# A mixture of experts with its matmuls turned, and gathers that leave out empty places

## The chip, the core and the metric

The kernel runs on one core of a Trainium2 chip. The metric is the device time of one execution in microseconds (us). TensorE (PE) multiplies and transposes, VectorE (DVE) and ScalarE (ACT) work on tiles element by element, GpSimd (POOL) here mostly issues indirect transfers, and SyncE (SP) issues the other transfers. SBUF is the on-chip memory of 128 partitions; PSUM is the memory that TensorE writes, in eight banks of 128 x 512 f32. A matmul has a stationary operand, which is loaded first, and a moving operand, whose columns stream past it.

## The reference, cut to what matters

The whole is a decoder of two layers on 4 x 256 tokens of width 256. The change lies in the feed-forward part of the first layer, a mixture of 64 experts: each token goes to the 6 experts with the largest scores, and every token also goes through one shared expert.

```python
E, K, H, F_EXP = (64, 6, 256, 176)
def _swiglu(x, g, v, o):
    return jax.nn.silu(x @ g) * (x @ v) @ o
scores = jax.nn.softmax(x @ w_router.T, axis=-1)
topw, topi = jax.lax.top_k(scores, K)
combine = jnp.zeros((T, E), x.dtype).at[jnp.arange(T)[:, None], topi].add(topw)
# over all experts: acc + cw[:, None] * _swiglu(x, g, v, o)
shared = _swiglu(x, swg, swv, swo)
return (routed + shared).reshape(b, s, h)
```

So 1024 x 6 = 6144 pairs of token and expert are worked. All of it is f32.

## The kernel before

The program is one block with a stream of instructions written out for each engine; counting semaphores hold the streams together. Up to the mixture the kernel does the first attention and a state-space scan; behind it come the rest of the first layer and the second layer.

The pairs are sorted into blocks of 128 places. Each expert owns at least one block, an expert with more than 128 tokens gets further ones behind. Four blocks make a group (`NJ = 4`). The first 16 groups (`FIXED`) hold block e of expert e; a loop behind them works the groups of overflow, of which this input has one. So 17 groups, or 68 blocks, are worked.

For a block, POOL gathers 128 rows of 1 KB from the normalized tokens in DRAM (`gather`, one row for each place, by the table `tok_of`; a place that no token fills reads row 0). TensorE turns the tile (`turn_g`, two transposes), ACT copies it to `xgT`. `gate_up` has the activations stationary and the weights moving: two matmuls of 352 columns give gate and value of 128 tokens, tokens on partitions. ACT takes a tanh of the gate, DVE's `hidden` makes silu(gate) x value out of it in two instructions. The result has tokens on partitions, and the down projection needs the hidden units there, so `turn_hid` transposes it (two transposes of 88 units), ACT copies it back, and `down` runs two matmuls of 256 columns. DVE copies the product to `y_out`, and SP stores it block by block to `y_dram`. The 68 blocks' rows are gathered from there, weighted and added later.

The weights stream in. SP has a ring of two groups: `load_block` for block j of group i + 2 is issued when block j of group i has been copied out, right behind the store of that block:

```python
for j in range(NJ):
    store_y(d * RING + r, j)
    sp.wait_ge(w_loaded[j], at(d, 32 * RING, 32 * (r + RING)))
    sp.sem_inc(load_due, 1)
    load_block(d * (RING * NJ) + ((r + RING) * NJ + j), j, w_gv[:, r * NJ + j], w_dn[:, r * NJ + j])
```

A block's weights are one transfer of 352 KB (`w_gv`) and one of 192 KB (`w_dn`, 96 partitions with 2 KB each, of which 88 carry data). The gather of group i + 2 is issued behind the turn of group i + 1, which TensorE does within group i. The engines also carry work of a later part within the groups (`side`, `rotate_key`).

Of the kernel before, what the change touches and what calls it, by code (L numbers as in the profile page):

```python
# [12 lines left out]
ALU = mybir.AluOpType  # L13
# [20 lines left out]
FH = F // 2  # L34
FP = 96
# [99 lines left out]
ACT_STEPS = 1 + PAIRS + 1  # L135

# [18 lines left out]
def build(nc, a, out):  # L155

    with ExitStack() as ctx:
# [124 lines left out]
        tok_id = sb("tok_id", [P, TILES])  # L282
        tri_bf = sb("tri_bf", [P, P], BF16)
# [51 lines left out]
        w_gv = sb("w_gv", [P, RING * NJ, KD, 2 * F])  # L335
        w_dn = sb("w_dn", [FP, RING * NJ, 2, D])
        y_out = sb("y_out", [P, NJ, D])
        g_th = sb("g_th", [P, NJ, F])
        hid = sb("hid", [P, NJ, F])
        hidT = sb("hidT", [FH, NJ, 2 * P])  # L340
        xg = sb("xg", [P, NJ, D])
        xgT = sb("xgT", [P, NJ, KD * P])
        sh_gv = sb("sh_gv", [P, KD, 2 * F])
        sh_dn = sb("sh_dn", [FH, 2, D])
# [130 lines left out]
        x_stored = sem("x_stored")  # L475
        gathered = [sem(f"gathered{j}") for j in range(NJ)]
        w_loaded = [sem(f"w_loaded{j}") for j in range(NJ)]
        y_stored = [sem(f"y_stored{j}") for j in range(NJ)]
# [3 lines left out]
        gv_ready = sem("gv_ready")  # L482
        g_tanh = sem("g_tanh")
        g_silu = sem("g_silu")
        hid_ready = sem("hid_ready")
        hid_turned = sem("hid_turned")
        hidT_copied = sem("hidT_copied")
# [57 lines left out]
        def pair(n):  # L545
            return ps[:, n:n + 2, :].rearrange("p a b -> p (a b)")

# [6 lines left out]
        def _(sp):  # L554
# [67 lines left out]
            for dst, src in ((w_router, "w_router"), (iota, "iota"), (tok_id, "tok_id"), (tri_bf, "tri_bf")):  # L622
                sp.dma_start(dst[:], a[src]).then_inc(moe_consts, 16)
            for dst, src in ((sh_gv, "sh_gv"), (sh_dn, "sh_dn"), (pos, "pos"), (ident_bf, "ident_bf"),
                             (x_wq, "x_wq"), (x_wo, "x_wo"), (head_sel, "head_sel")):
# [3 lines left out]
            def load_block(e, j, gv, dn):  # L629
                sp.dma_start(gv, a["w_gv"][bass.ds(e, 1)].rearrange("a p k n -> (a p) k n")).then_inc(w_loaded[j], 16)  # L630
                sp.dma_start(dn, a["w_dn"][bass.ds(e, 1)].rearrange("a p k n -> (a p) k n")).then_inc(w_loaded[j], 16)

            for r in range(RING):
                for j in range(NJ):
                    if r:
                        sp.wait_ge(w_loaded[j], 32 * r)
                    load_block(r * NJ + j, j, w_gv[:, r * NJ + j], w_dn[:, r * NJ + j])
# [25 lines left out]
            used = used_groups(sp)  # L663
            with sp.Fori(FIXED, used) as i:
                for j in range(NJ):
                    e = sp.value_load(expert_row[0:1, bass.ds(i * NJ + (j - E), 1)], min_val=0, max_val=E - 1)
                    buf = bass.ds((i & 1) * NJ + j, 1)
                    store_y(i - RING, j)
                    sp.wait_ge(w_loaded[j], at(i, 32, 0))
                    sp.sem_inc(load_due, 1)  # L670
                    load_block(e, j, w_gv[:, buf].rearrange("p a k n -> p (a k) n"),
                               w_dn[:, buf].rearrange("p a k n -> p (a k) n"))
            for r in range(RING):
                for j in range(NJ):
                    store_y(used - RING + r, j)
# [23 lines left out]
        def _(pe):  # L699
# [236 lines left out]
            pe.wait_ge(moe_consts, 64)  # L936
# [8 lines left out]
            def gate_up(j, x_of, w):  # L945

                for k in range(KD):
                    last = mm(ps[:, j, 0:2 * F], x_of(k), w(k), start=(k == 0), stop=(k == KD - 1))  # L948
                last.then_inc(gv_ready, 1)

            def turn_hid(n, j, bk):
                pe.wait_ge(hid_ready, n + 1)
                for f in range(2):
                    last = nc.tensor.transpose(ps[0:FH, bk, f * P:(f + 1) * P], hid[:, j, f * FH:(f + 1) * FH], ident[:])
                last.then_inc(hid_turned, 1)

            def down(n, j, bk, w):
                pe.wait_ge(hidT_copied, n + 1)
                for f in range(2):
                    last = mm(ps[:, bk, 256:512], hidT[:, j, f * P:(f + 1) * P], w(f), start=(f == 0), stop=(f == 1))  # L960
                last.then_inc(down_ready, 1)

            def shared_up(tiles):

                for t in tiles:
                    if t >= NJ:
                        pe.wait_ge(down_copied, t - NJ + 1)
# [1902 lines left out]
```

## Time and profile before

| | |
|---|---|
| three runs | 991.32, 992.77, 993.33 us; median 992.77 us |
| the profiled execution | span 985.7 us from the first to the last instruction; what lies around the span is not in the profile |
| TensorE | busy 870.2 us (88%) |
| VectorE, ScalarE, GpSimd | busy 720.6, 510.4, 407.1 us |
| the loop over the groups | 521.3 us to 698.7 us of the span |
| HBM | read 88.45 MB, written 17.14 MB |

The shares are means over parts with different limits, so the loop is read by itself. There the profile's row of DMA shows 9 tenths or more, and TensorE's row does too.

### The profile page before, as it was taken

Reading aid. Unit: us, or ns where it says so; the run is one execution under the profiler, and the core shown is the slowest. Engines: PE = TensorE matmul, PEld = TensorE weight load, DVE = VectorE, ACT = ScalarE, POOL = GpSimd, SP = SyncE. Lnnn points to the kernel's source line nnn. Section 1 sums busy time; section 2 is a strip of 40 time slices with the busy share of each in tenths; the row PEclk is TensorE's granted clock in tenths of the full one; section 3 lists DMA queues with packets and bytes.
Section 4 is the critical chain, followed back from the end, with each engine's and each line's share of the span. In section 5 each row is a group of like instructions: output and inputs, shape, how many; then the busy total and the mean of one; then the engine's idle time right before and its main releaser. Section 6 shows DMA issues by size and latency. Waiting matters only on the chain.

```text
span 985.7 us, 15418 instructions
## 1 busy us (share of the span) xinstructions
PE 870.2 (88%) x5267; PEld 568.3 (58%) x5271; DVE 720.6 (73%) x1377; ACT 510.4 (52%) x1022; POOL 407.1 (41%) x338
## 2 busy tenths in 40 slices
PE   7999999999999999988889999999546867899886
PEld 3466666666565666656666777677423654343443
DVE  5667786959696867768774556665467798998797
ACT  3563554545544444445444334455522457898485
POOL 0203448494848577534214333333377312221013
PEclk9999999999999999989999999999866998999998
DMA  5451212112131221100926999999633000000001
GB/s 189 153 196 27 65 49 86 70 65 77 58 102 53 81 75 65 44 1 1 238 94 216 298 311 310 313 312 303 179 96 98 26 1 3 5 8 6 1 6 38
DMA packets 54743, 106.46 MB, mean 108 GB/s; under 512 B 8909, under 2 KB 26645, under 8 KB 54165
## 3 DMA queue, kind: packets, MB, share of 16 engines
q1 hardware_dynamic: 48917, 89.88, 29.6%
q0 software_dynamic: 5760, 15.74, 6.0%
q8 instruction: 37, 0.61, 0.3%
q14 instruction: 29, 0.24, 0.1%
HBM read 88.45 MB, written 17.14 MB: 107 GB/s over the span
## 4 chain that ended last, share of the span: by engine, by line
PE 54%; DVE 19%; DMA 10%; issue 5%; ACT 5%; SPq 3%; POOL 3%; DVEq 0%; ACTq 0%; POOLq 0%
PE ps L777 10%; PE ps L715 6%; DMA w_dn<-in_w_dn 5%; PE ps L873 5%; PE ps L725 4%; DVE row_max L2696 3%; PE ps L948 3%; DMA y_dram<-y_out 3%; PE ps L1280 3%; POOL key_part L1507 2%; DVE state L2119 2%; PE ps L795 2%; PE ps L960 2%; DMA key_part<-y_dram,slot_idx 2%; PE ps L1266 2%
## 5 line engine op out<-in xcount | busy, mean ns | idle before, releaser
L1479 POOL DMA_INDIRECT xg<-x_dram,tok_of x68 | 65.1, 958 | 131.8 <-PE ps L1006 94.2
L777 PE MATMUL ps<-w_vg,xT 128*128 128x512 f32 x256 | 116.8, 597 | 1.2 <-DVE th L2162 1.2
L1429 POOL TENSOR_TENSOR state<-state,rows_bc 128x1024 f32<-128x1024 f32 x22 | 53.8, 2446 | 95.5 <-DVE state L2119 41.9
L715 PE MATMUL ps<-xT,w_qks 128*128 128x512 f32 x192 | 86.5, 596 | 5.2 <-ACT qT L1585 5.2
L948 PE MATMUL ps<-w_gv,xgT 128*128 128x352 f32 (+1 forms) x272 | 87.4, 464 | 2.5 <-DMA w_dn<-in_w_dn 2.4
L2696 DVE TENSOR_REDUCE row_max<-ps 128x4 f32<-128x1024 f32 x64 | 74.3, 1217 | 7.1 <-PE ps L1245 6.3
L2130 DVE TENSOR_TENSOR aT<-ps,tri 128x768 f32<-128x768 f32 x64 | 59.7, 954 | 27.0 <-PE ps L725 26.9
L1585 ACT ACTIVATE probT<-ps 128x512 f32<-128x512 f32 x128 | 69.5, 594 | 10.1 <-PE ps L1266 9.6
L777 PEld LDWEIGHTS ps<-w_vg,xT 128*128 128x128 f32 x256 | 45.8, 190 | 48.8 <-issue 43.1
L960 PE MATMUL ps<-w_dn,hidT 88*128 88x256 f32 (+1 forms) x272 | 70.0, 379 | 0.0
L948 PEld LDWEIGHTS ps<-w_gv,xgT 128*128 128x128 f32 x272 | 48.9, 190 | 27.0 <-issue 5.2
L715 PEld LDWEIGHTS ps<-xT,w_qks 128*128 128x128 f32 x192 | 34.9, 190 | 46.6 <-issue 36.4
L1422 POOL TENSOR_TENSOR drive<-du,rows_bc 128x1024 f32<-128x1024 f32 x26 | 61.0, 2361 | 0.1
L1585 ACT ACTIVATE v<-ps 128x256 f32<-128x256 f32 x64 | 24.5, 382 | 70.6 <-PE ps L777 70.3
L1507 POOL DMA_INDIRECT key_part<-y_dram,slot_idx x48 | 49.9, 1039 | 26.9 <-DMA y_dram<-y_out 12.6
L873 PE MATMUL ps<-w_o,oT 128*128 128x256 f32 x256 | 60.7, 386 | 0.3 <-DVE xres L2235 0.3
L2162 DVE SCALAR_TENSOR_TENSOR th<-th,ps 128x256 f32<-128x256 f32 x64 | 26.5, 417 | 44.7 <-ACT th L1585 44.0
L2468 DVE TENSOR_SCALAR y_out<-ps 128x256 f32<-128x256 f32 x68 | 28.7, 422 | 41.7 <-DMA y_dram<-y_out 26.7
L873 PEld LDWEIGHTS ps<-w_o,oT 128*128 128x128 f32 x256 | 48.1, 194 | 9.9 <-issue 4.2
L1433 POOL TENSOR_TENSOR y<-y,state 128x1024 f32<-128x1024 f32 x22 | 51.9, 2357 | 1.7
L1585 ACT ACTIVATE g_th<-ps 128x176 f32<-128x176 f32 x76 | 23.6, 317 | 54.6 <-PE ps L948 54.4
L2310 DVE SCALAR_TENSOR_TENSOR g_th<-g_th,ps 128x176 f32<-128x176 f32 x76 | 25.4, 335 | 35.5 <-ACT g_th L1585 34.7
(327 smaller groups left out, 2066.6 us busy)
## 6 DMA issues: line engine op xcount, KB each, us to landing
w_gv<-in_w_gv SPq DMA_DIRECT2D x68, 352.0 KB, 8.2
rows_bc<-x_dbl_dram SPq DMA_DIRECT2D x32, 512.0 KB, 3.8
w_dn<-in_w_dn SPq DMA_DIRECT2D x68, 192.0 KB, 9.6
y_dram<-y_out SPq DMA_DIRECT2D x68, 128.0 KB, 7.5
y_dram<-blank SPq DMA_DIRECT2D x4, 1408.0 KB, 13.2
w_vg<-in_wvg SPq DMA_DIRECT2D x8, 512.0 KB, 4.9
w_qks<-in_wqks SPq DMA_DIRECT2D x8, 384.0 KB, 3.1
w_o<-in_wo SPq DMA_DIRECT2D x8, 256.0 KB, 2.7
```

What stands on the lines that cost most here:

```text
L715: last = mm(bank(PJ + n % 2), w_qks[:, k, part * P:(part + 1) * P], xT[:, k, half * 512:(half + 1) * 512], start=(k == 0), stop=(k == KD - 1))
L777: last = mm(bank(PJ + t % 2), xT[:, k, t * P:(t + 1) * P], w_vg[:, k, :], start=(k == 0), stop=(k == KD - 1))
L873: last = mm(ps[:, X + b % 2, 256 * t:256 * t + 256], oT[:, h, c:c + P], w_o[:, h, :], start=(h == 0), stop=(h == 1))
L948: last = mm(ps[:, j, 0:2 * F], x_of(k), w(k), start=(k == 0), stop=(k == KD - 1))
L960: last = mm(ps[:, bk, 256:512], hidT[:, j, f * P:(f + 1) * P], w(f), start=(f == 0), stop=(f == 1))
L1422: G.tensor_tensor(drive_buf(m), du[:, e], b_row[:, n % 2], ALU.mult).then_inc(drive_ready, 1)
L1429: G.tensor_tensor(state_of(m), state_of(m), c_row[:, n % 2], ALU.mult).then_inc(read_out, 1)
L1479: G.indirect_dma_start(xg[:, j, :], None, x_dram, bass.IndirectOffsetOnAxis(ap=col, axis=0)).then_inc(gathered[j], 16)
L1507: G.indirect_dma_start(yg[:, n % 8, :], None, y_dram, bass.IndirectOffsetOnAxis(ap=slot_idx[:, n // TOPK, n % TOPK:n % TOPK + 1], axis=0)) ...
L1585: return nc.scalar.activation(out, in_, func, **kw)
L2130: return V.tensor_tensor(aT[:, 2 * b:2 * b + 2, :], ps[:, first_bank:first_bank + 2, 0:384], tri[:].unsqueeze(1).to_broadcast([P, 2, 384]) ...
L2696: V.tensor_reduce(row_max4[:, u, :, 4 * i + 2 * (b % 2):4 * i + 2 * (b % 2) + 2], src, AX.X, ALU.max).then_inc(unit_free, 1)
```

## The change

Gate and up projection are turned. The weights become the stationary operand and the 128 tokens the moving one, so the result has hidden units on partitions, as the down projection wants them: no transposes of the hidden tile and no copies of them. The 176 units are split into 112 (`FA`, a matmul each for gate and value) and 64 (`FB`; their gate and value stand in one matmul of 128 columns of weights, "low"). The 64-unit parts of two blocks lie in the lower and the upper half of the partitions of one tile, and their down matmuls have 64 rows each. ACT's Silu replaces tanh and one of DVE's two instructions. The tiles are worked by pairs of blocks: a copy, an activation or a product takes two blocks in one instruction, the outputs of a group are copied to SBUF in two instructions of 512 columns when the whole group is done, and they are stored two blocks at once with 2 KB for each partition (the rows of `y_dram` stand in another order, and `slot_idx` follows it). The stores and loads of a group therefore start when the group is done, no more block by block. The weights of a block come in three transfers (352, 112 and 64 KB). Last, `tok_of` holds 1024 for an empty place, and the gather skips every index above 1023; the tile is set to zero once, ahead of the loop.

```diff
-                sp.dma_start(gv, a["w_gv"][bass.ds(e, 1)].rearrange("a p k n -> (a p) k n")).then_inc(w_loaded[j], 16)
-                sp.dma_start(dn, a["w_dn"][bass.ds(e, 1)].rearrange("a p k n -> (a p) k n")).then_inc(w_loaded[j], 16)
+                sp.dma_start(w_up[:, r * NJ + j, :], a["w_up"][bass.ds(e, 1)].rearrange("a p n -> (a p) n")
+                             ).then_inc(w_loaded[j], 16)
+                sp.dma_start(w_dn[:, r * NJ + j, :], a["w_dn"][bass.ds(e, 1)].rearrange("a p n -> (a p) n")
+                             ).then_inc(w_loaded[j], 16)
+                first = HIGH * (j % 2)
+                sp.dma_start(w_low[first:first + FB, (r * NJ + j) // 2, :],
+                             a["w_low"][bass.ds(e, 1)].rearrange("a p n -> (a p) n")).then_inc(w_loaded[j], 16)
...
-            def store_y(i, j):
-                sp.wait_ge(down_copied, at(i, NJ, j + 1) + TILES)
+            def store_y(i, p):
+
+                sp.wait_ge(down_copied, at(i, 2, COPIED + 2))
                 sp.sem_inc(load_due, 1)
-                sp.dma_start(y_dram[bass.ds(i * (NJ * P) + j * P, P), :], y_out[:, j, :]).then_inc(y_stored[j], 16)
+                sp.dma_start(y_rows(i, p), y_pair(p)).then_inc(y_stored[p], 16)
...
-                    for j in range(NJ):
-                        store_y(d * RING + r, j)
-                        sp.wait_ge(w_loaded[j], at(d, 32 * RING, 32 * (r + RING)))
-                        sp.sem_inc(load_due, 1)
-                        load_block(d * (RING * NJ) + ((r + RING) * NJ + j), j, w_gv[:, r * NJ + j], w_dn[:, r * NJ + j])
+                    for p in range(2):
+                        store_y(d * RING + r, p)
+                        for j in (2 * p, 2 * p + 1):
+                            sp.wait_ge(w_loaded[j], at(d, LOADS * RING, LOADS * (r + RING)))
+                            sp.sem_inc(load_due, 1)
+                            load_block(d * (RING * NJ) + ((r + RING) * NJ + j), j, r)
...
+            def group(i, r):
...
+                for p in range(2):
+                    pe.wait_ge(xgT_copied, at(i, 2, p + 1))
+                    pe.wait_ge(hid_ready, at(i, 4, HIDDEN - 4 + p + 1))
+                    for o in range(2):
+                        j = 2 * p + o
+                        pe.wait_ge(w_loaded[j], at(i, LOADS, LOADS))
+                        up(ps[0:FA, p, 2 * o * P:(2 * o + 1) * P], w_of(j), "gate", x_of(j))
+                        last = up(ps[0:FA, p, (2 * o + 1) * P:(2 * o + 2) * P], w_of(j), "value", x_of(j))
+                    last.then_inc(up_ready, 1)
+                for p in range(2):
+                    pe.wait_ge(hid_ready, at(i, 4, HIDDEN - 4 + 2 + p + 1))
+                    for o in range(2):
+                        last = up(ps[:, 2 + p, o * P:(o + 1) * P], w_of(2 * p + o), "low", x_of(2 * p + o))
+                    last.then_inc(up_ready, 1)
+                pe.wait_ge(down_copied, at(i, 2, COPIED))
+                for p in range(2):
+                    pe.wait_ge(hid_ready, at(i, 4, HIDDEN + p + 1))
+                    for o in range(2):
+                        mm(ps[:, 4 + o, p * D:(p + 1) * D], hidT_a[:, 2 * p + o, :], w_dn[:, r * NJ + 2 * p + o, :],
+                           start=(p == 0), stop=False, skip_group_check=True)
+                    for o in range(2):
+                        turn_g(i + 1, 2 * p + o)
+                for p in range(2):
+                    pe.wait_ge(hid_ready, at(i, 4, HIDDEN + 2 + p + 1))
+                    for o in range(2):
+                        rows = slice(HIGH * o, HIGH * o + FB)
+                        last = mm(ps[:, 4 + o, p * D:(p + 1) * D], hidT_b[rows, p, :], w_low[rows, r * (NJ // 2) + p, :],
+                                  start=False, stop=True, skip_group_check=True)
+                last.then_inc(down_ready, 1)
...
             def gather(j, col):
-                G.indirect_dma_start(xg[:, j, :], None, x_dram, bass.IndirectOffsetOnAxis(ap=col, axis=0)
-                                     ).then_inc(gathered[j], 16)
+                G.indirect_dma_start(xg[:, j, :], None, x_dram, bass.IndirectOffsetOnAxis(ap=col, axis=0),
+                                     bounds_check=TOK - 1, oob_is_err=False).then_inc(gathered[j], 16)
...
-            V.tensor_copy(tok_of[:], ps[:, Y + 1, 0:COLS]).then_inc(route_vec, 1)
+            V.tensor_scalar(tok_of[:], ps[:, Y + 1, 0:COLS], float(TOK), None, ALU.add).then_inc(route_vec, 1)
...
+                dve.wait_ge(down_ready, at(i, 1, 3))
+                if not first:
+                    for p in range(2):
+                        dve.wait_ge(y_stored[p], at(i, 16, 0))
+                for o in range(2):
+                    V.tensor_copy(y_out[:, o::2, :], bank(4 + o).rearrange("p (a d) -> p a d", a=2)).then_inc(down_copied, 1)
```

On TensorE, within a group of the loop, the second half of a group stood as follows before. A row is a line, an operation, output<-moving and stationary operand, output size and count; ISA and REGISTER_ALU rows are waits and their arithmetic.

```order
L948 MATMUL ps<-w_gv,xgT 128x352 x2
L952 REGISTER_ALU
L954 MATMUL ps<-ident,hid 88x128 x2
L960 MATMUL ps<-w_dn,hidT 128x256 x2
L1004 ISA
L1006 MATMUL ps<-ident,xg 128x128 x2
```

Now the end of the up projection, the down projection and the turns of the next group stand there:

```order
L979 MATMUL ps<-xgT,w_up 128x128 x4
L1073 REGISTER_ALU
L1075 REGISTER_ALU
L1077 MATMUL ps<-w_dn,hidT_a 128x256 x2
L1045 ISA
L1047 MATMUL ps<-ident,xg 128x128 x4
L1075 REGISTER_ALU
L1077 MATMUL ps<-w_dn,hidT_a 128x256 x2
L1047 MATMUL ps<-ident,xg 128x128 x4
L1082 REGISTER_ALU
L1085 MATMUL ps<-w_low,hidT_b 128x256 x2
```

The transposes of the hidden tile are gone, the up matmuls have 128 columns in place of 352, all of them stand ahead of the first down matmul, and the turns of the next group stand two blocks together.

On SP, in the loop's body, one block's share was this, four times for a group:

```order
L651 DMA y_dram<-y_out 128x256
L630 ISA
L630 DMA w_gv<-in_w_gv 128x704
L631 ISA
L631 DMA w_dn<-in_w_dn 96x512
L649 REGISTER_ALU
```

Now two blocks share a store, and each block has three loads; the rows from the second on come a second time ahead of the next store:

```order
L673 DMA y_dram<-y_out 128x512
L646 ISA
L646 DMA w_up<-in_w_up 128x704
L648 ISA
L648 DMA w_dn<-in_w_dn 112x256
L651 ISA
L651 DMA w_low<-in_w_low 64x256
```

So a group has 14 transfers on SP's queue in place of 12, and all of them stand behind the wait for the whole group.

## Rows read from the trace of the kernel before

**Rows 1.** The page's head: busy engines, DMA share and rate in 40 slices of the span.

```profile
span 985.7 us, 15418 instructions
PE 870.2 (88%) x5267; PEld 568.3 (58%) x5271; DVE 720.6 (73%) x1377; ACT 510.4 (52%) x1022; POOL 407.1 (41%) x338
...
DMA  5451212112131221100926999999633000000001
GB/s 189 153 196 27 65 49 86 70 65 77 58 102 53 81 75 65 44 1 1 238 94 216 298 311 310 313 312 303 179 96 98 26 1 3 5 8 6 1 6 38
```

**Rows 2.** Busy time by stretch; last three columns: TensorE's clock, DMA share, GB/s.

```profile
46.00:56.00 10.00, 9.25 (x40) 4.75 (x38) 5.40 (x12) 7.11 (x13) 0.00 (x0) 1.00 1.09 386
...
480.00:490.00 10.00, 9.40 (x79) 6.70 (x78) 9.38 (x46) 8.32 (x35) 1.05 (x4) 1.00 1.06 270
...
520.50:531.50 11.00, 10.98 (x53) 8.19 (x54) 4.16 (x12) 5.77 (x15) 5.56 (x6) 1.00 0.35 96
...
541.40:641.40 100.00, 97.66 (x457) 71.04 (x456) 59.02 (x175) 41.88 (x123) 35.47 (x38) 1.00 1.06 309
```

**Rows 3.** DMA, 541.4 to 641.4 us: packets, MB, share; issues, KB, us to landing.

```profile
q1 hardware_dynamic: 14941, 25.74, 88.1%
q0 software_dynamic: 1882, 5.14, 17.7%
...
w_dn<-in_w_dn SPq DMA_DIRECT2D x39, 192.0 KB, 9.6
y_dram<-y_out SPq DMA_DIRECT2D x38, 128.0 KB, 8.2
xg<-x_dram,tok_of POOLq DMA_INDIRECT x38, 6.7
```

**Rows 4.** Chain that ended last, second group: start, us; a matmul counts twice.

```profile
531.49 3.55 PE ps L948 x12
...
535.26 1.19 PE ps L948 x4
...
536.66 0.86 PE ps L960 x4
537.53 0.22 PE ps L1006 x2
...
541.44 0.59 PE ps L948 x2
```

**Rows 5.** Timeline of TensorE: first up matmuls of first and last group.

```profile
521.27 3.81 PE L948 MATMUL ps<-w_gv,xgT 128*128 128x352 f32 x12
...
687.42 3.81 PE L948 MATMUL ps<-w_gv,xgT 128*128 x12
```

**Rows 6.** The chain elsewhere: f32 matmuls of 64 rows (L725), of 128 columns (L930).

```profile
190.27 0.88 PE ps L725 x8
...
464.79 0.44 PE ps L930 x4
```

**Rows 7.** Timeline of SP's queue: a store, two loads, the next store.

```profile
568.26 0.36 SPq L651 DMA_DIRECT2D y_dram<-y_out  x1
568.99 0.34 SPq L630 DMA_DIRECT2D w_gv<-in_w_gv  x1
569.52 0.35 SPq L631 DMA_DIRECT2D w_dn<-in_w_dn  x1
570.21 0.36 SPq L651 DMA_DIRECT2D y_dram<-y_out  x1
```

**Rows 8.** The chain at the loop's end: last copy, its store.

```profile
698.75 0.43 DVE y_out L2468
...
699.41 3.57 DMA y_dram<-y_out
```

**Rows 9.** DVE by line: busy, mean ns | idle before; 256 and 512 columns.

```profile
L2468 DVE TENSOR_SCALAR y_out<-ps 128x256 f32<-128x256 f32 x68 | 28.7, 422 | 41.7 <-DMA y_dram<-y_out 26.7 <-PE ps L960 14.2
...
L2235 DVE TENSOR_TENSOR xres<-xres,ps 128x512 f32<-128x512 f32 x32 | 21.4, 668 | 6.5 <-PE ps L873 6.5
```

**Rows 10.** Timeline of POOL: a gather that waits for nothing but the one ahead.

```profile
531.93 1.02 POOL L1479 DMA_INDIRECT xg<-x_dram,tok_of  x1 [0.30 <-issue]
```

More of the change, by code:

```diff
@@ L943, in _, with part_of, up @@
             last.then_inc(route_mm, 1)
-            def gate_up(j, x_of, w):
+            def part_of(w, k, part):
+                first = k * UP + dict(gate=0, value=FA, low=2 * FA)[part]
+                return w[:, first:first + (2 * FB if part == "low" else FA)]
+            def up(out, w, part, x_of):
                 for k in range(KD):
[L948 to L960, printed above, removed]
-                last.then_inc(down_ready, 1)
[L963 to L967, printed above, removed]
-                    gate_up(t % NJ, lambda k: xT[:, k, t * P:(t + 1) * P], lambda k: sh_gv[:, k, :])
@@ L970, in shared_down, with shared_up, x_of @@
-            def shared_down(tiles):
-                for t in tiles:
-                    turn_hid(t, t % NJ, t % NJ)
-                for t in tiles:
-                    down(t, t % NJ, t % NJ, lambda f: sh_dn[:, f, :])
-            pe.wait_ge(layer_loaded, 128)
-            shared_up(range(NJ))
+                    last = mm(out, part_of(w, k, part), x_of(k), start=(k == 0), stop=(k == KD - 1))
+                return last
+            Y_SH = (3, 2)
+            def shared_up(h):
+                def x_of(k):
+                    return xT[:, k, h * 512:(h + 1) * 512]
+                if h:
+                    pe.wait_ge(hid_ready, 2)
+                up(ps[0:FA, 0, :], sh_up, "gate", x_of)
+                up(ps[0:FA, 1, :], sh_up, "value", x_of).then_inc(up_ready, 1)
+                if h:
+                    pe.wait_ge(down_copied, 2)
+                up(bank(2), sh_up, "low", x_of).then_inc(up_ready, 1)
@@ new lines, in shared_down @@
+            def shared_down(h):
+                pe.wait_ge(hid_ready, 2 * h + 1)
+                if h:
+                    pe.wait_ge(down_copied, 2)
+                for t in (0, 1):
+                    mm(ps[:, Y_SH[0], t * D:(t + 1) * D], hidT_a[:, t, :], sh_dn[:], start=(t == 0),
+                       stop=False, skip_group_check=True)
+                pe.wait_ge(hid_ready, 2 * h + 2)
+                for t in (0, 1):
+                    mm(ps[:, Y_SH[1], t * D:(t + 1) * D], hidT_a[:, 2 + t, :], sh_dn[:], start=(t == 0),
+                       stop=False, skip_group_check=True)
+                for t in (0, 1):
+                    for n in range(2):
+                        rows = slice(HIGH * n, HIGH * n + FB)
+                        last = mm(ps[:, Y_SH[n], t * D:(t + 1) * D], hidT_b[rows, t, :], sh_low[rows, :], start=False,
+                                  stop=True, skip_group_check=True)
+                last.then_inc(down_ready, 1)
@@ L1818, in xgT_of @@
-            def xgT_of(i, j, first):
-                act.wait_ge(xg_turned, at(i, NJ, j + 1))
+                f(blk_hot[:, t % 2], blk_hot[:, t % 2], ACT.Copy, scale=tok_far[:, t:t + 1]).then_inc(hot_scaled, 1)
+            nc.scalar.preload_act_table_set("silu_and_others")
+            silu_shared(0)
+            scale_probs()
+            keep_shared(0)
+            scale_hot(0)
+            silu_shared(1)
+            for t in range(1, TILES):
+                scale_hot(t)
+            act.wait_ge(angle, 8)
@@ L1840, in cast_key @@
+                for p in range(2):
+                    act.wait_ge(up_ready, at(i, 4, HIDDEN + 2 + p + 1))
+                    f(silu_b[HIGH:P, 2 * p:2 * p + 2, :].rearrange("p a b -> p (a b)"),
+                      ps[0:FB, 2 + p, 0:2 * P], ACT.Silu).then_inc(silu_ready, 1)
+                for p in range(2):
+                    xgT_of(i + 1, p)
+                if side:
+                    side(2)
+                    side(3)
             def cast_key(j, q):
```

280 lines of the change are left out of this document (141 added, 139 removed).

## The prediction

> **What bounds it now.** I read the page's head first. In the slices of the loop over the groups the DMA engines show 9 tenths and 298 to 313 GB/s [rows 1], and a stretch of 100 us inside it shows a DMA share of 1.06 at 309 GB/s while TensorE is busy 97.66 us of 100 [rows 2]. Two resources are full there, so I ask which one paces. The chain of waits gives TensorE's own need: three blocks' up matmuls 3.55, the fourth 1.19, a down projection 0.86, two transposes 0.22 [rows 4]. That is 4 x 1.19 + 4 x 0.86 + 8 x 0.22 = 9.96 us a group, and the second group took just that, 541.44 - 531.49 = 9.95 [rows 4]. From 541.44 to the start of the seventeenth at 687.42 lie 14 groups, 10.43 each [rows 4, 5]. The other side: a group moves 4 x (352 + 192 + 128 + 128) KB = 3.28 MB, at 309 GB/s 10.6 us [rows 2]. So DMA paces all but the first two groups, with TensorE half a microsecond behind. While those two run on weights loaded ahead the DMA share starts at 0.35 [rows 2]. The weights' last transfer takes 9.6 us from issue to landing, the stores 8.2 [rows 3]: a full queue. The clock is at its upper level, granted 1.00, in all these stretches [rows 2].
>
> **TensorE's part.** Every f32 matmul stands twice in the rows (two passes). Four passes of 128 columns, each with weights of its own, take 0.44 us, 0.11 each [rows 6]; that is the shape of the new up matmuls. 24 of them make 48 x 0.11 = 5.28 us. The down matmuls over 112 units stay 256 columns long, 0.43 each as now: 1.72 for four. The 64-row parts lie in opposite halves of the partitions. The attention has such pairs: four passes of 256 and four of 128 columns, eight recorded passes on the chain, take 0.88 us [rows 6]; two passes of 256 (0.43) and two of 128 (0.22) for each half make 0.65 a half, 1.30 in a row, so 0.88 says that most of the halves run beside each other. Four 64-row matmuls then cost between 0.86 and 1.72; I take 0.9 to 1.2, say 1.0. Turns: 8 x 0.11 = 0.88. Sum 8.9 us, against 9.96; bounds 8.7 and 9.6.
>
> The Trainium skill, "TensorE: Matmul & The Clock Gate", section "Back-to-back issue gap", speaks against this gain: in a stream of weight loads and matmuls the spacing follows both, 81 ns at 128 columns where columns alone give about 56. Taking those 25 ns on top of the columns as an estimate, a pass would cost 0.135 us and the group about 10.1; the 0.11 of this trace, weight loads in the stream, decides against it.
>
> **DMA's part.** A block's weights fall from 544 to 352 + 112 + 64 = 528 KB, the padding rows. The stores stay 128 KB. Of the 68 x 128 = 8704 places 6144 hold a token, so if skipped places move nothing a gather falls from 128 to 90 KB. A group: 4 x (528 + 128 + 90) KB = 3.06 MB, at 309 GB/s 9.9 us. Nothing in the trace shows a skipping gather. Bounds: it saves nothing (4 x 784 KB, 10.4 us), or the rest runs faster too: 386 GB/s was reached with stores of 1 KB rows, but weight loads alone ran at 270 [rows 2], so I count on no more than 325, 9.4 us.
>
> **The new order.** All stores and loads of a group wait for its end. Two copies of 512 columns (0.67 each by the nearest line [rows 9]) and the hand-overs put SP's first issue about 1.9 us behind TensorE's last matmul. SP spaces transfers by 0.73, 0.53 and 0.69 [rows 7]; 14 take about 8.5 us, less than a period. The last weights of group i + 2 land at A behind the end of group i. With 9.9 us of transfers from 1.9 on, and 1.3 to land, A is 13. TensorE needs them behind three quarters of the first up matmuls, 2.6 us into group i + 2, and has 6.3 left then. Two periods being A + 6.3, the period by this ring is (13 + 6.3) / 2 = 9.7. The queue's 9.9 is larger, by little; two limits this close seldom both stay at their mean, and I take 10.0.
>
> The second store of a group is now behind two blocks of weights in the queue, and both copies of the next group wait for it. It is issued 1.9 + 4.2 = 6.1 us behind a group's end and may take 4 us before the copies wait. With a queue that runs empty once a period I count 4.5, which is in the 10.0.
>
> POOL: gathers follow each other by 1.02 + 0.30 = 1.3 us [rows 10]. The turns now come by twos, so the fourth gather starts some 3.9 us behind the first turn, lands within 6.7 [rows 3], and is wanted one period behind the fourth turn, which comes 1.7 us behind the first: 11.7 against 10.6. Covered by 1 us.
>
> DVE and ACT get fewer, wider instructions; both stay below a period and I count nothing.
>
> **The sum.** Groups 0 and 1 run on TensorE: 2 x 8.9. Group 2 waits for its ring: it ends 13 + 6.3 behind the end of group 0, so it lasts 10.4. Fourteen more at 10.0, and 1 us since the last group's loads read their expert's number first: 17.8 + 10.4 + 140 + 1 = 169.2. Before: 521.27 to 698.75, 177.5 [rows 5, 8]. Gain 8.3. Behind the loop the last copy of 0.43 becomes two of 0.67, and where one block was left to store (3.57 from issue to landing [rows 8]) four are: 0.9 + 0.7 for SP's next issue + 0.4 for more bytes, a loss of 2.0. Ahead of the loop the shared expert loses 16 transposes, 1.8 us, and gains columns, beside the routing; between 0 and -1.8 I take -0.5. Sum: -8.3 + 2.0 - 0.5 = -6.8. The profiled span of 985.7 becomes 978.9. The runs' median of 992.77 lies 7.1 above that span; I carry that over: 986.0 us.
>
> **The rivals.** *Packets, not bytes.* 14941 packets carried 25.74 MB [rows 3]. A block now has 128 + 112 + 64 rows of weights and 64 longer rows stored, 368 for 352. If packets set the time, that queue's share of 88.1 rises by 4.5%, while the gathers' 17.7 falls by 29%: the period is 10.43 x 0.987 = 10.3, the sum 4.2 us worse, 990. Against it: 1 KB rows alone ran at 386 GB/s [rows 2]. A gather that saves nothing ends at the same place, a period of 10.4 and 991.6. The Trainium skill, "DMA: Bandwidth & Descriptors", section "Bandwidth", says that transfers under 64 KB are dominated by their descriptors and asks for 1 MiB; the pieces of 64 KB are what it warns of, and no row here times one.
>
> *Late loads, slower than before.* If the store takes its present 8.2 us [rows 3] rather than 4.5, the copies wait for it about 4 us after the group's end, every load moves back by about 3.5, and A is 16.5: period 11.4, 14 x 1.4 = 20 us more than forecast, 1006. For it: DVE already waits 26.7 us for stores at that copy [rows 9]. Against it: the 8.2 comes of a queue that never empties, and a longer period empties it. It decides at a period of 10.5, where the forecast's gain is gone: A = 14.7, a store that takes 6 us.
>
> *TensorE paces.* If the DMA engines do better than by bytes, as they may with fewer rows on POOL's queue, the period falls to 9.2: 14 x 0.8 = 11 us less, 975.
>
> **How the numbers follow.** Forecast, a period of 9.6 to 10.2: 0.52, 980 to 989. Packets or an idle skip: 0.15, 989 to 993. Late loads: 0.20, 993 to 1010. TensorE paces: 0.13, 972 to 980. This kernel's runs can tell about 0.2%, 2 us. Below 990.8 lie the forecast, the last case and a fifth of the packets: 0.68. Within 2 us: 0.12. Above: 0.20. The range of 976 to 998 leaves out a third of the last case and half of the late loads, under 0.2.
>
> **What would show it.** Up matmuls of 0.22 us each and 64-row pairs together in 0.43 to 0.6; no DVE wait of more than 1 us for the stores; group starts 9.6 to 10.2 apart from the fourth on; DMA share still about 1; POOL's queue down by three tenths in MB. The prediction is wrong if the DMA share falls well below 1 while TensorE waits for weights (the ring), if the gathers' MB do not fall, or if a gather is what TensorE waits for.

## The result, and the profile after

The change makes the kernel slower. Median 1007.04 us (998.11 to 1012.17, four runs) against 992.05 us. The ratio of the medians is 1.0151; the ratio worked out from the fast runs is 1.0188, with a 95% interval of 1.0141 to 1.0235 that holds both. The forecast was 986.0 us, so it has the wrong sign. The profile is that of the slowest of the four executions (1012.17 us).

The head of the page of the profiled execution answers to [rows 1]:

```profile
span 1010.3 us, 15907 instructions
...
PE 874.4 (87%) x5651; PEld 595.2 (59%) x5655; DVE 706.1 (70%) x1303; ACT 484.3 (48%) x900; POOL 412.3 (41%) x339
...
PE   7999999999999999987978888988635885899886
...
PEclk9999999999999999988899889999857898999998
DMA  5450112221211212103627988998433100000001
GB/s 185 167 174 26 63 47 94 76 87 47 85 68 66 85 45 66 38 0 100 176 94 220 269 241 254 280 287 237 164 100 96 42 1 3 6 7 7 1 6 37
```

Before, TensorE's row and the row of its granted clock (PEclk, in tenths) read:

```profile
PE   7999999999999999988889999999546867899886
...
PEclk9999999999999999989999999999866998999998
```

Where the slices inside the loop (the 22nd to the 28th) showed 9 tenths for TensorE, and from the 23rd on for DMA too, at 298 to 313 GB/s, both rows now have holes, DMA moves 237 to 287 GB/s in the 23rd to the 28th, and the clock row, which had 9 throughout, shows 8 in three slices of the loop (the 23rd, the 24th and the 29th, with which it ends). Neither engine that was full is full now: something makes them wait for each other. The next view is busy time by stretch (its last three columns are clock, DMA share and GB/s; [rows 2] is the same view of before).

```profile
541.40:641.40 100.00, 86.68 (x615) 76.75 (x614) 44.78 (x123) 25.38 (x55) 36.61 (x36) 0.93 0.93 268
537.00:539.00 2.00, 2.00 (x21) 2.00 (x20) 0.42 (x1) 0.38 (x1) 1.14 (x2) 1.00 0.57 159
539.00:541.00 2.00, 2.00 (x19) 1.97 (x18) 1.00 (x3) 0.89 (x3) 0.00 (x0) 1.00 0.75 169
...
572.70:578.00 5.30, 5.30 (x25) 5.30 (x26) 1.00 (x3) 0.76 (x2) 0.00 (x0) 0.50 1.01 306
```

In the same 100 us TensorE is busy 86.68 us for 97.66, at a DMA share of 0.93 for 1.06. The last row is a stretch granted 0.50, TensorE's lower level of 1.2 GHz, inside the loop. TensorE's timeline says where such stretches come from. In it the bracket is the idle time ahead of a row and what ended it:

```profile
535.30 5.54 PE L979 MATMUL ps<-xgT,w_up 128*112 128x128 f32 x48
540.67 1.03 PE L1077 MATMUL ps<-w_dn,hidT_a 112*128 112x256 f32 x4
...
544.44 2.00 PE L979 MATMUL ps<-xgT,w_up 128*112 128x128 f32 x16
548.06 1.10 PE L979 MATMUL ps<-xgT,w_up 128*112 128x128 f32 x8 [1.62 <-DMA w_low<-in_w_low]
550.15 2.92 PE L979 MATMUL ps<-xgT,w_up 128*112 128x128 f32 x24 [0.99 <-DMA w_low<-in_w_low]
...
570.52 1.10 PE L979 MATMUL ps<-xgT,w_up 128*112 128x128 f32 x8 [1.74 <-DMA w_low<-in_w_low]
572.69 5.46 PE L979 MATMUL ps<-xgT,w_up 128*112 128x128 f32 x24 [1.07 <-DMA w_low<-in_w_low]
```

```profile
705.01 2.25 PE L979 MATMUL ps<-xgT,w_up 128*112 128x128 f32 x16
...
712.61 5.46 PE L979 MATMUL ps<-xgT,w_up 128*112 128x128 f32 x24 [2.69 <-DMA w_low<-in_w_low]
...
720.86 1.13 PE L1085 MATMUL ps<-w_low,hidT_b 64*128 64x256 f32 x8
```

The first two rows are a group that waits for nothing: 48 passes of the up projection in 5.37 us (535.30 to 540.67), and the next group 9.14 us behind (544.44). That next group stops behind 16 and behind 24 passes, 1.62 and 0.99 us, each time for `w_low`, the last of a block's three loads, and takes 12.2 us, to the next start at 556.67. At 570.52 and 572.69 the same waits are 1.74 and 1.07 us long, and the 24 passes behind them take 5.46 us where they took 2.92: this is the stretch at 0.50. In the profile of the loop TensorE waits 17 times for `w_low`, and the copy of the outputs waits 6 times for a store (columns: total, times, longest):

```profile
PE ps L979 <- DMA w_low<-in_w_low: 22.5, 17, 2.7
...
DVE y_out L2550 <- DMA y_dram<-y_out: 13.5, 6, 3.6
```

The groups now come in pairs, one of 9.1 to 10.1 us and one of 12.2 to 15.3. From the third group (544.44) to the seventeenth (705.01) a period is 160.57 / 14 = 11.47 us, where it was 10.43 [rows 4, 5]. The loop lasts from 525.12 to 721.99, 196.9 us for 177.5.

Why are the loads late? SP's timeline gives the first and last issue of a group (two rows of fourteen), the chain of waits the way of the last load from issue to landing, here of the first group and of the third:

```profile
537.01 0.36 SPq L673 DMA_DIRECT2D y_dram<-y_out  x1
...
544.94 0.47 SPq L651 DMA_DIRECT2D w_low<-in_w_low  x1
```

```profile
544.94 5.17 DMA w_low<-in_w_low
...
566.24 6.40 DMA w_low<-in_w_low
```

The first group ends at 535.35 us, the first store is issued at 537.01, the last load at 544.94, and it lands at 550.15: A, the time from a group's end to its last landing, is 14.8 us. For the third group it is 572.69 - 556.67 = 16.0. The forecast had 13. Issues and landings of the changed kernel beside [rows 3]:

```profile
q1 hardware_dynamic: 14905, 23.55, 80.1%
q0 software_dynamic: 1595, 3.22, 12.6%
...
y_dram<-y_out SPq DMA_DIRECT2D x18, 256.0 KB, 4.1
...
w_low<-in_w_low SPq DMA_DIRECT2D x34, 64.0 KB, 4.9
xg<-x_dram,tok_of POOLq DMA_INDIRECT x36, 4.6
```

The gathers move 3.22 MB in 36 transfers, 89 KB each, where 38 moved 5.14 MB: the bytes of skipped places are really not moved.

### The profile page after: what moved, and what is told of

It reads as the page before. It is cut to its first block, busy times and chain, and to the rows that moved or that the text cites. A ratio compares the mean times of both kernels' runs of the same rounds, so it can differ in the third digit from the quotient of the medians.

```text
span 1010.3 us, 15907 instructions
## 1 busy us (share of the span) xinstructions
PE 874.4 (87%) x5651; PEld 595.2 (59%) x5655; DVE 706.1 (70%) x1303; ACT 484.3 (48%) x900; POOL 412.3 (41%) x339
## 3 DMA queue, kind: packets, MB, share of 16 engines
q0 software_dynamic: 5760, 12.60, 4.5%
## 4 chain that ended last, share of the span: by engine, by line
PE 57%; DVE 18%; DMA 7%; issue 5%; ACT 5%; SPq 5%; POOL 2%; DVEq 0%; ACTq 0%; POOLq 0%
PE ps L803 10%; PE ps L741 6%; PE ps L979 5%; PE ps L899 5%; DMA w_low<-in_w_low 4%; PE ps L751 4%; DVE row_max L2780 3%; PE ps L1339 2%; PE ps L1147 2%; DVE state L2185 2%; PE ps L821 2%; PE ps L1325 2%; PE ps L1077 2%; SPq L651 1%; SPq L646 1%
## 5 line engine op out<-in xcount | busy, mean ns | idle before, releaser
L979 PE MATMUL ps<-xgT,w_up 128*112 128x128 f32 (+1 forms) x816 | 111.4, 299 | 23.6 <-DMA w_low<-in_w_low 22.5
L1540 POOL DMA_INDIRECT xg<-x_dram,tok_of x68 | 69.8, 1027 | 148.2 <-PE ps L1047 96.0
L979 PEld LDWEIGHTS ps<-xgT,w_up 128*112 128x112 f32 (+1 forms) x816 | 104.1, 201 | 33.3 <-issue 16.2
L1646 ACT ACTIVATE probT<-ps 128x512 f32<-128x512 f32 x128 | 69.5, 594 | 10.1 <-PE ps L1325 9.5
L2533 DVE TENSOR_TENSOR hidT_a<-silu_a,ps 112x256 f32<-112x256 f32 x34 | 14.2, 419 | 67.1 <-ACT silu_a L1646 66.4
L1646 ACT ACTIVATE silu_a<-ps 112x256 f32<-112x256 f32 (+1 forms) x36 | 14.2, 396 | 85.7 <-PE ps L979 82.6
L2550 DVE COPY y_out<-ps 128x512 f32<-128x512 f32 x34 | 21.9, 686 | 27.9 <-DMA y_dram<-y_out 13.5
L2185 DVE TENSOR_TENSOR_SCAN state<-decay,drive 128x1024 f32<-128x1024 f32 x18 | 40.7, 2277 | 0.0
```

The source lines that it names most:

```text
L979: last = mm(out, part_of(w, k, part), x_of(k), start=(k == 0), stop=(k == KD - 1))
L1540: G.indirect_dma_start(xg[:, j, :], None, x_dram, bass.IndirectOffsetOnAxis(ap=col, axis=0), bounds_check=TOK - 1, oob_is_err=False).then_ ...
L1646: return nc.scalar.activation(out, in_, func, **kw)
L2185: V.tensor_tensor_scan(state_of(m), decay[:, m % 2], drive_buf(m), 0.0, ALU.mult, ALU.add).then_inc(scanned, 1)
```

## The experiments

All ratios are to executions of the kernel before that were timed along with the run. The period is that of the third to the seventeenth group, worked out as above; the last column is the time from the loop's first up matmul to the first gather that brings outputs back (182.7 us before, 202.5 in the changed kernel). Period and last column come from one profiled execution each.

| run | ratio (95%) | period, us | loop to first return, us |
|---|---|---|---|
| changed kernel, first time | 1.0188 (1.0141 to 1.0235) | 11.47 | 202.5 |
| changed kernel, again | 1.0121 (1.0069 to 1.0172) | 11.04 | 191.6 |
| stores ahead of the loads | 1.0178 (1.0126 to 1.0230) | 11.30 | 201.4 |
| 12 unread matmuls a group | 1.0293 (1.0256 to 1.0329) | 11.82 | 208.7 |
| 6 unread matmuls a group | 1.0126 (1.0083 to 1.0170) | 10.75 | 189.9 |
| up weights early | 1.0100 (1.0063 to 1.0136) | 10.71 | 191.2 |
| split waits | 1.0055 (1.0024 to 1.0085) | 10.43 | 185.5 |
| early and split | 0.9980 (0.9952 to 1.0007) | 9.77 | 178.2 |
| early and split, no skip | 1.0021 (0.9996 to 1.0046) | 9.81 | 182.3 |
| early, split, overflow early, fourth turn late | 0.9874 (0.9833 to 0.9915) | 9.52 | 168.9 |
| before, with the skip | 1.0006 (0.9980 to 1.0032) | 10.32 | 180.1 |
| before, loads at the group's end | 1.0218 (1.0185 to 1.0251) | 11.64 | 201.2 |

The theory was that the loads come late because all of them start at a group's end; the rivals were the wait for the stores, a slower queue (packets), and a clock that falls for a reason of its own.

**Up weights early.** TensorE is done with a group's up weights 3.8 us ahead (540.67 and 544.44) of the group's end, so their next load can start there.

```diff
+sp.wait_ge(up_ready, at(d * RING + r, 4, HIDDEN + 4))
+sp.sem_inc(load_due, 1)
+for j in range(NJ):
+    sp.wait_ge(w_loaded[j], at(d, LOADS * RING, LOADS * (r + RING)))
+    sp.sem_inc(load_due, 1)
+    load_block(d * (RING * NJ) + ((r + RING) * NJ + j), j, r, "up")
 for p in range(2):
     store_y(d * RING + r, p)
...
+for j in range(NJ):
+    sp.sem_inc(load_due, 1)
+    load_block(d * (RING * NJ) + ((r + RING) * NJ + j), j, r, "down")
```

> The changed kernel, in which SP issues the four loads of the up weights (352 KB each) of group i + 2 as soon as TensorE has done the up matmuls of group i, ahead of the two stores; the eight smaller loads follow the stores. Late loads (my theory): in the changed kernel TensorE idles 22.5 us for the last small load of a block, because every load waits for the group's end and the last one lands some 15 us behind it. Two thirds of the bytes now start about 3.5 us before a group's end, the rest is done about 10 us behind it: the waits for weights fall below 5 us, the granted clock stays at 1.00 in the loop, the period of a group falls from 11.5 to 10.0, and the time to 0.985 to 1.000 of the kernel before. Rival, DMA engines do worse with more and smaller transfers: the DMA share stays at 1.06 all the time, the period is 10.8 or more, the ratio 1.005 to 1.015. Rival, the copies' wait for the stores is the cause: ratio 1.015 to 1.02, as without the edit.

Half right. TensorE's waits for `w_low` are 13.4 us, where they were 22.5 in the first profile of the changed kernel and 17.6 in the second, and they were to fall below 5. The ratio, 1.0100, cannot be told from the repeated run of the changed kernel (1.0121):

```profile
PE ps L987 <- DMA w_low<-in_w_low: 13.4, 11, 2.8
...
PE ps L1055 <- DMA xg<-x_dram,tok_of: 9.8, 8, 3.7
```

Four of those for `w_low` (1.85 to 1.97 us, at 565.37, 587.49, 631.33 and 652.85) now stand ahead of a group's first block, whose up matmuls do not read `w_low`: the one semaphore of a block counts its three loads. The longest, 2.8 us, is in the overflow group, whose loads this edit leaves as they were. The other row is the gather; 4.8 us of it lie ahead of the loop's first group.

**Stores first.** Both stores ahead of the twelve loads.

```diff
 for p in range(2):
     store_y(d * RING + r, p)
-    for j in (2 * p, 2 * p + 1):
+for j in range(NJ):
...
```

> The changed kernel, in which SP issues both stores of a group ahead of the twelve loads. Late loads: DVE's 13.5 us of waits for the stores at the copy go, which lets SP start about 2 us earlier in the six groups that waited, but the last load still is the fourteenth transfer behind a group's end: gain of 2 to 7 us on the changed kernel, ratio to the kernel before 1.012 to 1.017. Rival, the wait for the second store is what makes the loads late (the rival of the prediction as it stood there, 3.5 us in every group): the period falls to 10.0 and the ratio to 1.000 or below.

The copies no longer wait for a store at all, yet the ratio stays. TensorE's waits are 19.5 us for 22.5:

```profile
PE ps L979 <- DMA w_low<-in_w_low: 19.5, 23, 2.6
```

So the copies' wait for the stores is not what makes this kernel slow.

**Unread matmuls.** They fill TensorE's waits (in the second run 4 and 2 of them).

```diff
+for n in range((0, 0, 8, 4)[j]):
+    mm(ps[:, 3, D:D + P], ident[:], xgT[:, 0, 0:P], start=True, stop=True)
 pe.wait_ge(w_loaded[j], at(i, LOADS, LOADS))
```

> The changed kernel, in which TensorE works 8 matmuls of 128 columns that nobody reads ahead of its wait for the third block's weights and 4 ahead of the fourth's, 2.6 us of added work a group, most of it where it now idles. If its idle stretches are what lets the granted clock fall to 0.50 in the loop (about 11 us lost in the profiled run: 24 passes took 5.46 in place of 2.91), the clock stays at 1.00, the ring of weights sets the period as before, 10.6 to 11.0, and the time falls by 5 to 11 us: ratio to the kernel before 1.007 to 1.014. Rival, the clock falls for another reason: the stretches at half clock stay, and the added work shows where no wait covers it, ratio 1.02 to 1.04.

> The changed kernel with half of the added work of the earlier filled run: 4 unread matmuls ahead of the wait for the third block's weights and 2 ahead of the fourth's, 1.3 us a group, so a group needs 10.4 us of TensorE. If waits of 1.5 us and more are what lets the clock fall, most stretches at half clock go and the period comes near the ring's 10.6 to 11: ratio to the kernel before 1.005 to 1.013. Rival, the fall has nothing to do with the waits: as many stretches at half clock as without, ratio 1.015 to 1.03.

The same stretch of the loop in the two runs, twelve first:

```profile
545.00:690.00 145.00, 145.00 (x1181) 134.67 (x1180) 67.91 (x169) 41.95 (x90) 51.99 (x51) 1.00 0.93 259
```

```profile
545.00:690.00 145.00, 143.52 (x1136) 130.61 (x1135) 73.73 (x187) 48.00 (x103) 54.70 (x54) 1.00 0.99 285
```

The clock stays at 1.00 in both (0.93 in the changed kernel over this stretch). With twelve TensorE has no idle time left and its own work paces, at 11.8 us a group: my time for this run was wrong, since it forgot that the groups without waits pay for the fill too. With six a group has 1.3 us more to do, waits almost nothing, and its period is 10.75, less than in either profile of the changed kernel; the time is level with the second of them (1.0126 and 1.0121). The clock thus falls because TensorE waits: filled, the waits no longer let it fall. With six, the added work costs no more than the waits did.

**Split waits.** A semaphore of its own for the two smaller loads, waited for ahead of the down matmuls; with the loads at the group's end, and with the early ones.

```diff
-LOADS = 48
+LOADS, DOWN = 16, 64
...
 for p in range(2):
+    pe.wait_ge(down_loaded[p], at(i, DOWN, DOWN))
     pe.wait_ge(hid_ready, at(i, 4, HIDDEN + p + 1))
```

> The changed kernel with the split waits alone: the up matmuls wait for the up weights, the down matmuls for the two smaller loads, but all stores and loads still start when the group has been copied. The last up weights are two transfers (1.1 us) ahead of the last load and are needed at the same place, so the ring gives (14 + 6.4) / 2 = 10.2 in place of 10.6 to 11.2; the down weights are needed 3 us later and wait for nothing. Late loads: TensorE's waits fall to about half, period 10.2 to 10.6, ratio to the kernel before 1.000 to 1.010. Rival, the split alone does what the split with early loads did: ratio 0.995 to 1.000. Rival, only the start of the loads counts: ratio 1.012 to 1.02.

> The kernel of the run with early up weights, in which moreover TensorE's up matmuls wait for the up weights alone (a semaphore of its own for the two smaller loads of a block, waited for ahead of the down matmuls). With the loads early, TensorE still idled 13.9 us in the profile, nearly all for the last small load of the first block, which the up matmuls do not read. Late loads: with that gone no group waits for weights, the granted clock stays at 1.00, the period goes from 10.73 to 9.9 to 10.2 (bytes at 305 GB/s), the ratio to the kernel before is 0.995 to 1.002. Rival, the smaller transfers themselves move less per us (packets): DMA share at 1.05 or more without a gap and a period of 10.5 or more, ratio 1.005 or above. Rival, the fourth gather is what TensorE waits for next (1.2 us at two of the groups with the early loads): period 10.3 to 10.6 with a DMA share under 0.95, ratio 1.000 to 1.006.

Split alone gives 10.43 (the ring, worked out anew, gave 10.2); both together give 9.77 and take back all that the change lost. So lateness was made of two parts, when a load starts and how many loads a matmul waits for. What is left in the run with both:

```profile
PE ps L1063 <- DMA xg<-x_dram,tok_of: 8.1, 9, 1.8
...
PE ps L995 <- DMA w_up<-in_w_up: 4.0, 2, 2.7
```

```profile
682.09 1.10 PE L995 MATMUL ps<-xgT,w_up 128*112 128x128 f32 x8 [1.23 <-DMA w_up<-in_w_up]
685.91 4.55 PE L995 MATMUL ps<-xgT,w_up 128*112 128x128 f32 x24 [2.73 <-DMA w_up<-in_w_up]
```

The fourth gather (the third rival; 6.7 of the 8.1 us lie within the groups), and the overflow group, where SP reads each expert's number ahead of its loads: 1.23 and 2.73 us of waiting, and half clock behind.

**No skip.** The same kernel, gathers of all places.

> The same kernel with gathers of all 128 places. If its period is set by bytes, 0.15 MB more at 305 GB/s are 0.5 us a group, 7 us in the loop, 0.007 in the ratio above the run with split waits. If a skipped place costs the queue what a place costs, or if no byte limit paces, the two agree within 0.003.

**The skip alone**, on the kernel before.

> The kernel before with one part of the change alone: the gathers skip the places that no token fills. By bytes a group falls from 3.28 to 3.13 MB, at 309 GB/s from 10.43 to about 10.1 us, 14 groups save 4 to 6 us: ratio 0.994 to 0.996. Rival, a skipped row costs the queue what a row costs (both kernels show 5760 packets on POOL's queue): the period stays at 10.43 and the ratio within 0.998 to 1.002.

The skip takes the period from 9.81 to 9.77 and from 10.43 to 10.32 us: 0.04 and 0.11 us a group, against 0.5 and 0.3 by bytes. The first two times differ by 0.4%, but of the 4.1 us between their loops 3.6 lie behind the start of the last group; the other pair is level. The skip saves bytes and, in these profiles, hardly any time in the groups.

**Loads at the group's end, on the kernel before.**

```diff
+sp.wait_ge(down_copied, at(d * RING + r, NJ, NJ) + TILES)
 for j in range(NJ):
     store_y(d * RING + r, j)
```

> The kernel before with one part of the change alone: SP starts the stores and loads of a group when all four blocks of the group have been copied, no more block by block. If it is this order alone that makes the loads late, TensorE waits for weights in the loop, 1 us or more a group, and the ratio is 1.01 or above. By the ring (last load 15 us behind a group's end, needed 5 us into the group after next, a period of 9.9 to 10.2) it costs little here, since the old order wants the fourth block's weights late: ratio 1.000 to 1.006. Then the lateness comes of this order together with all the up matmuls at a group's head.

2.2% slower, against my price by the ring. Here the chain is the other one:

```profile
DVE y_out L2470 <- DMA y_dram<-y_out: 47.0, 29, 2.7
...
PE ps L956 <- DVE hid L2316: 10.5, 10, 1.8
PE ps L950 <- DMA w_dn<-in_w_dn: 8.1, 8, 1.7
```

DVE stands 47.0 us at the copies for stores that now start late, and what is behind the copy on DVE, the hidden tiles of the next blocks, is late for TensorE. So in the kernel before the order alone costs 2.2%. In the changed kernel, taking it back together with the shared semaphore is worth 1.4 to 2.1% (1.0121 and 1.0188 to 0.9980); which wait passes the lateness on differs.

**All of it, and the end of the loop.** Early and split, and three moves: the overflow group's up weights start behind the up matmuls of group 14, that group's stores go to ACT's queue, and the fourth turn stands behind the last down matmul.

> The kernel with early up weights and split waits, and three more moves: the loads of the overflow group start behind the up matmuls of group 14, ahead of that group's stores, which go to ACT's queue; and the fourth turn of the next group stands behind the last down matmul. In the profile of early loads with split waits the last group took 15.1 us, 4 of them waits for its up weights and 1.6 for half clock behind them, and the fourth gather held TensorE 0.7 to 1.2 us in some groups. With both gone the last group takes 9.5 to 11, the period 9.3 to 9.7, the loop is 5 to 9 us shorter: ratio to the kernel before 0.989 to 0.994. Rival, DMA by bytes (3.06 MB at 309 GB/s, 9.9 us a group) is what holds the period at 9.75: only the last group's 5 us come, ratio 0.993 to 0.996.

The ratio of 0.9874 is below the forecast of 0.989 to 0.994, but its interval reaches to 0.9915 and the ratio of the medians is 0.9902: faster than the kernel before, by about what was forecast. The three moves were not run one by one. Its loop, its DMA, the last group, and the copies' wait:

```profile
541.40:641.40 100.00, 97.89 (x764) 87.26 (x763) 54.27 (x144) 32.78 (x71) 44.71 (x44) 1.00 1.01 310
```

```profile
DMA packets 19089, 30.98 MB, mean 310 GB/s; under 512 B 3250, under 2 KB 10442, under 8 KB 19085
```

```profile
677.46 2.87 PE L993 MATMUL ps<-xgT,w_up 128*112 128x128 f32 x24
680.70 2.92 PE L993 MATMUL ps<-xgT,w_up 128*112 128x128 f32 x24 [0.38 <-DMA w_up<-in_w_up]
...
687.09 1.13 PE L1100 MATMUL ps<-w_low,hidT_b 64*128 64x256 f32 x8
```

```profile
DVE y_out L2567 <- DMA y_dram<-y_out: 39.2, 13, 4.9
```

TensorE is busy 97.89 us of 100 again, at a DMA share of 1.01, where it was 97.66 and 1.06 before the change [rows 2]. The last group takes 688.2 - 677.46 = 10.8 us for 17.0, and of the waits for the fourth gather 0.16 us are left within the groups. The copies wait 39.2 us for stores, more than the 13.5 in the changed kernel, and TensorE stays busy all the same: a long wait on an engine with time to spare is not yet a cost.

**The changed kernel again.**

> The changed kernel once more, beside the others on one chip: ratio to the kernel before 1.014 to 1.024 as in its first runs. The stretches at half clock in the loop follow waits of TensorE for weights of 1.5 us or more; if a profile shows fewer of them, its time is shorter by 1.6 to 2.9 us for each. At the router ahead of the loop, the half clock of the first profile (2.9 us) comes and goes, as it did in the other runs.

1.0121: below the range expected, its interval overlapping that of the first time. In its profile the loop begins with groups of 13.7 and 16.0 us and goes over to 10.0 to 10.8 from the tenth on. It is one program with two rhythms; that its runs spread from 993 to 1012 us because of them is likely and not shown, since two executions were profiled. The expectation's reading that the stretches at half clock follow waits of 1.5 us or more does not hold in the first profile: see the last section.

## Why the prediction was wrong

**The step that failed** is the ring: "With 9.9 us of transfers from 1.9 on, and 1.3 to land, A is 13." Its first part held: SP's first issue came 1.66 us behind the end (537.01 - 535.35) and fourteen transfers took 8.4 us to issue (537.01 to 545.41). The transfers did not run at 309 GB/s from the first one on: the queue had emptied, and the DMA share was 0.57 and 0.75 in the first four us (159 and 169 GB/s, windows above). That is 0.66 MB in place of 1.24, or 1.9 us at 309 GB/s, about the 1.8 by which the first group's A lies above 13. The last load was left 3.2 us from issue to landing (13 less 1.9 less the 7.9 from first to last issue) and took 5.2 and 6.4; in the last 3 us of each the next group's stores and loads were already issued (from 547.24 and 569.61 on), and what they took of it is not separated. With A at 14.8 to 16.0 and 6.5 us left behind the landing (550.15 to 556.67) the same formula gives (14.8 + 6.5) / 2 = 10.7 to 11.3. The run with six unread matmuls, which keeps the clock up, shows 10.75, though with 10.4 us of work a group it is no sharp test. The prediction named A = 14.7 as the place where the gain is gone, and A was there. Its sign for a failing ring came too: a DMA share of 0.93 while TensorE waits for weights.

**A term that was missing**: the clock. In the fourteen groups, passes behind waits took 5.46, 6.74, 4.55 and 4.55 us where 2.91, 3.9, 2.91 and 2.91 are usual: 8.7 us, 0.6 a group. The 11.47 measured less 0.6 is 10.85, which lies where the ring puts it. So of the 1.44 us a group above the forecast (140.4 / 14 = 10.03) about 0.8 are the ring and 0.6 the clock, by this estimate. The Trainium skill, "TensorE: Matmul & The Clock Gate", section "HAM oscillation — how this bites in real kernels", describes a kernel whose waits for DMA let the clock fall again for every tile; this trace agrees in kind (five such stretches behind waits for weights in its loop), and the prediction should have priced it as soon as a case had TensorE waiting.

**The late-load rival** had 0.20, and its time of 1006 us is what came, by another mechanism. It laid 3.5 us a group on the copies' wait for the second store. That wait was 13.5 us in all, the store landed in 4.1 us (4.5 forecast), and without the wait the time stayed. So the rival's time was met by luck. In the kernel before, with the loads put at the group's end, the copies do wait long for stores (47.0 us), and there I had priced the order at next to nothing.

**TensorE's part was right.** 9.14 us a group for 8.9 (bounds 8.7 to 9.6): 5.37 for 5.28 of up matmuls, 0.112 a pass, and 1.07 us for the 64-row pairs (543.37 to 544.44), for 1.0. The estimate of 0.135 a pass, worked out from the Trainium skill, "TensorE: Matmul & The Clock Gate", section "Back-to-back issue gap", is not borne out.

**DMA's part** was right on what moves (89 KB a gather for 90) and on its bounds of 9.4 to 10.4: the best version runs at 9.52, its fourteen groups moving 41.55 MB at 312 GB/s (2.97 MB a group for the 3.06 counted). Three readings in it were off, and the outcome does not hang on them: the 270 GB/s were not weight loads alone, since a store of 1024 KB to `x_dram` is issued in that stretch; packets are more than rows, about 426 a block for 388 before (14905 / 35 and 14941 / 38.5), not 368 for 352; and the rival's factor of 0.987 comes out as 0.989. The rival of packets is out: 19089 packets there in 100 us against 14941 + 1882 [rows 3], pieces of 64 and 112 KB among them, at the same rate.

**The ends of the loop.** The last group was forecast at 11.0 and took 17.0 (705.01 to 721.99): value loads between the loads, both stores ahead of them, and half clock behind the wait of 2.69 us; with the loads moved ahead it took 10.8. The first group lost 1.0 us to the clock that the sum had at nothing: TensorE waits 3.09 and 1.27 us for gathers ahead of it, the clock is 0.50 from 524 to 526 us, and its 48 passes take 6.58 for 5.54. The tail's loss was 0.4 us for 2.0, from the end of the last down matmul (before: from the start of the copy right behind it) to the first return gather, 5.18 before and 5.58 after. The shared stage was forecast at -0.5; the loop began 3.85 us later in the profile. Some 3 us of it are the router's matmuls, at half clock in one profile and not in another, whichever kernel it is (the stretch ahead of the routing, changed kernel and then stores first):

```profile
470.00:480.00 10.00, 8.61 (x43) 7.97 (x43) 3.73 (x10) 2.39 (x4) 3.46 (x9) 0.63 0.81 240
```

```profile
470.00:480.00 10.00, 9.04 (x53) 7.38 (x54) 5.38 (x19) 3.18 (x11) 2.96 (x8) 0.83 0.88 248
```

With the upper row's clock (0.63) the loops start at 525.12 us, with the lower's (0.83, as before the change) at 520.52; the seven profiles of the changed kernel and its variants at 0.83 or 0.84 have it between 519.76 and 522.62, where it was 521.27 before.

**The base** was wrong by chance of execution: the median's 7.1 us above the profiled span were carried over as something outside of it. An execution's time is 1.9 us above its span (1012.17 and 1010.3); the rest was the difference between executions of the kernel before, 983 to 996 us in later runs. In ratios nothing hangs on it.

By terms, in the profiles: loop 196.9 for 169.2 forecast, 27.7 too long = 20.2 in fourteen groups (160.6 for 140.4) + 6.0 in the last + 1.5 in the first two (19.3 for 17.8).

## What to carry to other kernels

Moving loads to the end of a batch is a change of its own, however many instructions it saves: follow one buffer from "free" through issue and landing to its reader, with the landing time of a full queue and a slow start of an empty one, and compare twice the wished period with it. Issue a load where its buffer becomes free and wait for it where it is read, each part by a semaphore of its own. If the sum leaves TensorE waiting at all, price half clock behind the wait too, as something that may come.

## What the runs showed of the hardware that was not expected

Two short waits with little work between can be enough to let the clock fall: 1.74 us, 1.10 us of matmuls, 1.07 us, and then 0.50 for some 5 us. The length of the waits alone does not tell when. In the changed kernel's profile two waits of 2.10 and 0.84 us, a little longer together, left the clock at 1.00, and two of 1.25 and 0.58 us were followed by 24 passes in 4.55 us, at 0.63 on average:

```profile
620.27 1.10 PE L979 MATMUL ps<-xgT,w_up 128*112 128x128 f32 x8 [2.10 <-DMA w_low<-in_w_low]
622.21 2.91 PE L979 MATMUL ps<-xgT,w_up 128*112 128x128 f32 x24 [0.84 <-DMA w_low<-in_w_low]
...
641.23 1.10 PE L979 MATMUL ps<-xgT,w_up 128*112 128x128 f32 x8 [1.25 <-DMA w_low<-in_w_low]
642.91 4.55 PE L979 MATMUL ps<-xgT,w_up 128*112 128x128 f32 x24 [0.58 <-DMA w_low<-in_w_low]
```

So a wait can be priced with half clock behind it as a risk, not as a rule; what decides is open.

Gathers that skip three places in ten take 1.03 us of POOL's time each instead of 0.96 (0.97 in the changed kernel's variant without the skip), and the queue shows 5760 packets for the whole kernel with and without the skip, for 12.60 and 15.74 MB; what a skipped place costs the queue stays open. So does why the changed kernel settles into its shorter rhythm in some executions.
